# Gated attention with a routed expert layer: one wait on counts dropped for the first batch's scatters, and VectorE's root of the variance moved ahead of the low halves of the expert weights

## The chip, the cores and the metric

The kernel runs on 1 core of one Trainium2 chip. The metric is the time on the device in microseconds (us). The engines are TensorE (PE in the profile; PEld is its weight load), VectorE (DVE), ScalarE (ACT), GpSimd (POOL) and SyncE (SP). Each has its own queue of instructions, and semaphores order the engines among each other. An instruction that finishes can count a semaphore up, and another engine's instruction waits until the count is reached.

## What is computed

Eight batches of 512 tokens with 256 channels. A layer norm gives xn. One branch is an attention over channels, the other a mixture of experts (32 experts, 8 groups of which 3 are kept, 6 experts for each token) with a shared expert:

```python
xn = _layernorm(x, axis=-1)
s = _L0_attn_ref(xn, Wq, Wk, Wv, Wo)         # scores of channels x channels, softmax, times V, times Wo
g = _silu(_L0_ffn_ref(xn, gate, w1, w2, w3, sw1, sw2, sw3))
x = x + s * g
# in _L0_ffn_ref: y = sum over experts of ce * (silu(x @ w1.T) * (x @ w3.T)) @ w2.T, plus the shared expert
```

## The kernel before, in words

The program has two stages. In the **first stage** it goes batch by batch (b = 0 to 7). For each batch it does the norm, the attention, the shared expert, the choice of the six experts of each token and the slot of each copy of a token in a table in DRAM (`slots_d`). GpSimd then copies the tokens to their slots: 24 scatters for a batch (4 tiles of tokens times 6 ranks), 192 in all, each an indirect DMA of 128 rows. In the **second stage** the experts run over pairs of slot tiles, the results go back to `slots_d`, and gathers bring them together again.

The order on each engine in the first stage is written out by hand. What matters here, with the names of the semaphores:

- **TensorE, batch(b)**: shared_up(0); product `s_a_ps`; shared_up(1) (`s_ab_ps`); turn(b+1) (`s_xt_ps`, line 685); product `s_s_ps` (scores); gate(b+1) (`s_lg_ps`, line 698); half 0 of the shared expert's output (`s_y_ps`, line 726); product with Wo (`s_r_ps`, line 710); half 1 (`s_y_ps`, line 726); wait for ScalarE's copy of r; product with V's weights (`s_m_ps`, line 710); gram(b+1) (`s_g_ps`, line 732); count(b+1) (`s_cnt`, lines 704 and 705); wait for ScalarE's copy of m; the attention's output (`s_at_ps`, line 726).
- **ScalarE, batch(b)**, in its later part: split_high(b+1) (line 539; it waits until the scatters of batch b-1 have landed, because they read the buffer that it writes); y half 0 (line 598); copy of r (line 602); y half 1 (line 598) and its DMA; normal(b+2, 0) (line 527; it waits for `s_rstd`, which VectorE counts in moved_mean); copy of m (line 610); normal(b+2, 1); copy of the gram (line 568); copies of the output (line 619); high_weights(b).
- **VectorE, batch(b)**: the two hidden products (line 1044); the maximum of the scores; spread_of(b+2); then route(b+1), split_low(b+1), low_weights(b-1) (line 1050: 12 instructions), spread_root(b+2) (lines 887 to 890), moved_mean (line 898), place(b+1) (lines 947 to 989; it waits for `s_cnt` of b+1 and ends with the slots of b+1, `s_slots`), weigh(b+1).
- **GpSimd** waits for `s_slots` of the batch, for the zeros that SyncE writes into the batch's slots (`s_first_pads`, `s_pads`), and for `s_split` of the tile. Before scatter n of a batch it calls `let_pass(b, n)`, which for some n waits until TensorE has reached a count: n = 2 `s_lg_ps`, 4 `s_y_ps`, 7 `s_r_ps`, 9 `s_y_ps`, 11 `s_m_ps`, 13 `s_cnt`, 15 `s_at_ps`, 17 `s_ab_ps`, 19 `s_a_ps`, 21 `s_xt_ps`. No data of the scatter depends on these waits.

Of the kernel before, what the change touches and what calls it, by code (L numbers as in the profile page):

```python
# [80 lines left out]
def turns(p):  # L81

    return sum(q <= p for q in PE_PAIRS)
# [10 lines left out]
def gated_attention_moe(nc, x, wq, wk_, wvT, wo, gwT, wexp, sw13T, sw2T, out):  # L94
    with ExitStack() as ctx:
# [29 lines left out]
        def chunks(v, c=HC):  # L125
            return v.rearrange("p (c n) -> p c n", c=c)
# [175 lines left out]
        def weights_of(b, low):  # L302
            return w16[:, b * (EB * 2 * WEXP):(b + 1) * (EB * 2 * WEXP)].rearrange(
                "p (e c) -> p e c", e=EB)[:, :, low * WEXP:(low + 1) * WEXP]

        def raw_weights(b):
            return w_all[:, (b + 1) * (EB * WEXP):(b + 2) * (EB * WEXP)].rearrange("p (e c) -> p e c", e=EB)
# [14 lines left out]
        def rank_of(at):  # L322

            return at - at % TOP_K + TOP_K - 1 - at % TOP_K
# [118 lines left out]
        @block.gpsimd  # L443
        def _(pool):
            pool.memset(ident[:], 0.0).then_inc(s_const, 1)
            pool.memset(pad[:], 0.0).then_inc(s_const, 1)
            pool.memset(tri[:], 1.0).then_inc(s_const, 1)
            pool.memset(ones[:], 1.0).then_inc(s_const, 1)
            for r in (restart, restart4, restart8):
                pool.memset(r[:], 1.0).then_inc(s_const, 1)  # L450
            pool.iota(pair_i[:], pattern=[[2 * P, EARLY]], base=3 * P, channel_multiplier=0)
            pool.iota(tile_i[:], pattern=[[P, 3]], base=0, channel_multiplier=3 * P).then_inc(s_const, 1)
            pool.wait_ge(s_const, 8)
            pool.affine_select(out=ident[:], in_=ident[:], compare_op=ALU.not_equal, fill=1.0,
                               base=0, pattern=[[-1, P]], channel_multiplier=1).then_inc(s_const, 1)

            pool.affine_select(out=tri[:], in_=tri[:], compare_op=ALU.is_gt, fill=0.0,
                               base=0, pattern=[[1, P]], channel_multiplier=-1).then_inc(s_const, 1)
            for r, n in ((restart, 1 + E), (restart4, 1 + TB), (restart8, 1 + GROUPS)):
                pool.memset(r[:].rearrange("p (t e) -> p t e", e=n)[:, :, 0:1], 0.0).then_inc(s_const, 1)  # L460


            def let_pass(b, n):

                nxt = b + 1 < B
                due = {4: (s_y_ps, 2 * b + 1), 7: (s_r_ps, b + 1), 9: (s_y_ps, 2 * b + 2),
                       11: (s_m_ps, b + 1), 15: (s_at_ps, 2 * b + 2)}
                if nxt:
                    due.update({2: (s_lg_ps, b + 2), 13: (s_cnt, b + 2), 17: (s_ab_ps, HC * b + HC + 1),
                                19: (s_a_ps, b + 2), 21: (s_xt_ps, 2 * b + 6) if b + 2 < B else (s_a_ps, b + 2)})  # L470
                else:
                    due[2] = (s_s_ps, b + 1)
                if n in due:
                    pool.wait_ge(*due[n])

            for b in range(B):
                pool.wait_ge(s_slots, b + 1)
                if b >= 1:
                    pool.wait_ge(s_pads[b], 16)
                for t in range(TB):  # L480
                    pool.wait_ge(s_split, b * TB + t + 1)
                    if b == 0:
                        pool.wait_ge(s_first_pads[t], 16)
                    for k in range(TOP_K):
                        at = b * BATCH_ROWS + t * TOP_K + k
                        let_pass(b, t * TOP_K + k)
                        pool.indirect_dma_start(slots_d[:, :], bass.IndirectOffsetOnAxis(ap=slot_at[:, at:at + 1], axis=0),  # L487
                                                split[b % XN_RING][:, t, :], None).then_inc(s_disp[b % XN_RING], 16)


            for k in range(XN_RING):
                pool.wait_ge(s_disp[k], 16 * BATCH_ROWS * (B // XN_RING))
            pool.sem_inc(s_scattered, 1)
            stored = 0
            for at in range(GATHERS):
                pages = at + E
                complete = min(-(-pages // 2), PAIRS)
                for pair in range(stored, complete):
                    pool.wait_ge(s_store[pair % DEEP], 16 * (pair // DEEP + 1))
                stored = complete  # L500
                if at >= GATH_RING:
                    pool.wait_ge(s_acc, at - GATH_RING + 1)
                ahead = at // 2 + 18 + SOON
                if at % 2 == 0:
                    pool.wait_ge(s_ehT_ps, min(ahead, PAIRS))
                else:
                    pool.wait_ge(s_eT_ps, turns(min(ahead + SOON + 1, PAIRS - 1)))
                pool.indirect_dma_start(gath[:, at % GATH_RING, :], None, slots_d[:, :],  # L508
                                        bass.IndirectOffsetOnAxis(ap=slot_at[:, rank_of(at):rank_of(at) + 1], axis=0)
                                        ).then_inc(s_gath[at % GATH_RING], 16)  # L510
# [354 lines left out]
        def _(dve):  # L865
# [8 lines left out]
            def spread_of(b):  # L874
                dve.wait_ge(s_x[b], 16)
                for t in range(TB):
                    ins = dve.bn_stats(stats[:, t, :], rows_of(b)[:, t * H:(t + 1) * H])  # L877
                then(ins)
                if b >= 1:
                    dve.wait_ge(s_xn, b * TB)  # L880
                for t in range(TB):
                    ins = dve.bn_aggr(mv[:, t, :], stats[:, t, :])
                ins.then_inc(s_var, 1)
# [13 lines left out]
            def moved_mean():  # L897
                dve.scalar_tensor_tensor(shift[:], mv[:, :, 0], -1.0, rstd[:], ALU.mult, ALU.mult).then_inc(s_rstd, 1)
# [133 lines left out]
            def table_row():  # L1032
                dve.wait_ge(s_table_ps, 1)
                dve.tensor_copy(w_packed.bitcast(I16), ps[0:1, 5, 0:2 * WORDS]).then_inc(s_tables, 1)
# [7 lines left out]
            def hidden(b, m):  # L1042
                dve.wait_ge(s_silu, b * HC + m + 1)
                dve.scalar_tensor_tensor(hT_s[:, m, :], ps[:, 5 + 2 * m, :], 1.0 / (X_UP * W_UP), silu_s[m],
                                         ALU.mult, ALU.mult).then_inc(s_h, 1)

            def low_part(low, raw, high):
                for c in range(WEXP // PART):
                    part_of = slice(c * PART, (c + 1) * PART)
                    ins = dve.scalar_tensor_tensor(low[:, part_of], raw[:, part_of], W_UP, high[:, part_of],  # L1050
                                                   ALU.mult, ALU.subtract)
                ins.then_inc(s_wlo, 1)

            def low_weights(b):
                dve.wait_ge(s_whi, b + 1)
                for e in range(EB):
                    low_part(weights_of(b, 1)[:, e], raw_weights(b)[:, e], weights_of(b, 0)[:, e])
# [6 lines left out]
            def batch(b):  # L1064
                hidden(b, 0)
                hidden(b, 1)
                dve.wait_ge(s_s_ps, b + 1)
                dve.tensor_reduce(mx[:], chunks(ps[:, 0, :]), AX_X, ALU.max).then_inc(s_mx, 1)
                dve.wait_ge(s_mx, b + 1)
                dve.tensor_scalar(nmx[:], mx[:], -SCALE, None, ALU.mult).then_inc(s_nmx, 1)  # L1070
                if b == 0:
                    weigh(0)
                if b + 2 < B:
                    spread_of(b + 2)
                elif b + 2 == B:
                    full_pairs()
                dve.wait_ge(s_ex, b * HC + HC)
                dve.reciprocal(rinv[:], rsum[:]).then_inc(s_ri, 1)
                if b == B - 1:
                    low_weights(b - 1)  # L1080
                    page_table()
                    low_weights_last(0)
                    table_row()
                    low_weights_last(1)
                    return
                route(b + 1)
                split_low(b + 1)
                if b >= 1:
                    low_weights(b - 1)
                if b + 2 < B:  # L1090
                    spread_root(b + 2)
                    moved_mean()
                place(b + 1)
                weigh(b + 1)

# [105 lines left out]
```

## Time and profile before

| what | us |
|---|---|
| median of 3 runs (lowest to highest) | 686.68 (683.47 to 690.63) |
| profiled execution, its own time | 691.99 |
| span of the profiled execution | 690.2 |
| TensorE, VectorE, ScalarE, GpSimd busy | 548.6, 472.2, 359.1, 383.4 |
| TensorE's mean granted clock, as a share | 0.922 |

All times in the rows below are of the profiled execution, counted from the start of its span. What lies around the span is 1.8 us. A row of the timeline gives start, duration, engine, line, operation, what is written and read, how many instructions were merged into the row, and in brackets how long the engine stood idle before it and which work ended that ("issue" when the profile shows nothing that it waited for, "remote" when the release isn't one that the profile can place).

### The profile page before, as it was taken

How to read it: one execution, taken by the hardware profiler on the slowest of the kernel's cores; microseconds unless marked ns; L12 is line 12 of the kernel's file. 1: busy time of each engine (PE TensorE's matmuls, PEld its weight loads, DVE VectorE, ACT ScalarE, POOL GpSimd, SP SyncE). 2: the span in 40 equal slices, each digit the busy share in tenths (PEclk: the TensorE clock that was granted, in tenths of full speed). 3: DMA queues.
4: the chain of work that ended last, by engine and by line, in shares of the span. 5: the costliest groups of instructions: out<-in, count | busy, mean ns of one | idle time of the engine just before them, and what ended most of it. 6: DMA issues, size and time to landing. Idle time of an engine off the chain costs nothing.

```text
span 690.2 us, 14473 instructions
## 1 busy us (share of the span) xinstructions
PE 548.6 (79%) x4095; PEld 446.7 (65%) x4095; DVE 472.2 (68%) x1443; ACT 359.1 (52%) x606; POOL 383.4 (56%) x402
## 2 busy tenths in 40 slices
PE   7789696979697978437999889888888889888830
PEld 6566575756576765326999777777777777677620
DVE  6968687877788877722454567667677667667765
ACT  5546464546464644224655656556556556556421
POOL 1156667676666766753003556556565556565662
PEclk9889798998898999868999999999999999999975
DMA  9999996858393532754888888888888988888764
GB/s 320 416 354 347 366 334 227 285 214 298 130 334 113 207 117 91 230 150 122 201 217 262 290 280 283 280 280 285 290 272 292 279 279 267 290 276 286 226 198 141
DMA packets 111288, 174.80 MB, mean 253 GB/s; under 512 B 25072, under 2 KB 68848, under 8 KB 110320
## 3 DMA queue, kind: packets, MB, share of 16 engines
q1 hardware_dynamic: 87280, 108.29, 47.4%
q0 software_dynamic: 18432, 50.36, 23.2%
q10 hardware_dynamic: 5504, 15.24, 6.4%
q8 instruction: 40, 0.66, 0.4%
q14 instruction: 32, 0.26, 0.1%
HBM read 78.41 MB, written 92.27 MB: 247 GB/s over the span
## 4 chain that ended last, share of the span: by engine, by line
PE 53%; DVE 21%; issue 15%; another core or an unknown queue 6%; ACT 4%; DMA 1%; DVEq 0%; SPq 0%; ACTq 0%
PE ps L835 17%; PE ps L857 8%; PE ps L726 7%; PE ps L710 6%; PE ps L818 6%; PE ps L718 4%; DVE sw L1133 3%; PE ps L845 3%; PE ps L732 2%; DVE w_all L1050 2%; DVE work L1152 2%; DVE work L1159 1%; DVE stats L877 1%; DVE early L1141 1%
## 5 line engine op out<-in xcount | busy, mean ns | idle before, releaser
L508 POOL DMA_INDIRECT early<-slots_d,slot_at x192 | 186.6, 972 | 178.0 <-DMA slots_d<-early 56.6
L487 POOL DMA_INDIRECT slots_d<-early,slot_at x96 | 96.9, 1009 | 75.0 <-issue 25.7
L487 POOL DMA_INDIRECT slots_d<-work,slot_at x96 | 97.7, 1018 | 45.1 <-issue 26.5
L835 PE MATMUL ps<-w_all,xnT 128*128 x798 | 102.9, 275 | 15.9 <-issue 13.6
L835 PEld LDWEIGHTS ps<-w_all,xnT 128*128 128x128 f16 x798 | 71.4, 98 | 36.3 <-issue 24.6
L647 ACT ACTIVATE xnT<-ps 128x1024 f16<-128x1024 f16 x67 | 68.8, 1029 | 46.6 <-PE ps L818 28.0
L668 ACT ACTIVATE early<-ps 128x512 f32<-128x512 f32 x112 | 67.3, 602 | 46.6 <-remote 30.8
L818 PE MATMUL ps<-ident,work 128*128 128x128 f16 x796 | 66.7, 222 | 24.9 <-issue 24.8
L1159 DVE CAST work<-ps 128x256 f16<-128x256 f32 x75 | 31.6, 422 | 75.0 <-remote 45.0
L1133 DVE SCALAR_TENSOR_TENSOR sw<-early,wk,sw 128x256 f32<-128x256 f32 x160 | 77.7, 486 | 3.5
L818 PEld LDWEIGHTS ps<-ident,work 128*128 128x128 f16 x796 | 54.6, 99 | 28.8 <-issue 26.4
L653 ACT ACTIVATE work<-ps 128x256 f32<-128x256 f32 x112 | 43.9, 393 | 55.6 <-remote 37.9
L857 PE MATMUL ps<-w_all,work 128*128 x447 | 62.6, 277 | 0.9 <-issue 0.9
L1152 DVE SCALAR_TENSOR_TENSOR work<-ps,work 128x256 f32<-128x256 f32 x112 | 46.5, 416 | 20.4 <-ACT work L653 19.0
L710 PE MATMUL ps<-early,work 128*128 128x256 f32 x128 | 39.4, 462 | 25.8 <-ACT work L533 18.9
L835 PE MATMUL ps<-w_all,sw 128*128 x396 | 50.6, 274 | 8.3 <-issue 8.0
L710 PEld LDWEIGHTS ps<-early,work 128*128 128x128 f32 x128 | 28.6, 231 | 34.7 <-ACT work L533 21.0
L726 PE MATMUL ps<-work,early 128*128 128x256 f32 x128 | 34.7, 432 | 17.7 <-issue 13.8
L857 PEld LDWEIGHTS ps<-w_all,work 128*128 128x128 f16 x447 | 43.9, 99 | 6.3 <-issue 1.5
L835 PEld LDWEIGHTS ps<-w_all,sw 128*128 128x128 f16 x396 | 35.4, 98 | 18.6 <-issue 12.7
L647 ACT ACTIVATE sw<-ps 128x1024 f16<-128x1024 f16 x33 | 34.0, 1032 | 20.9 <-remote 15.4
L718 PE MATMUL ps<-xnT,sw 128*128 128x512 f16 x192 | 44.0, 379 | 0.0
(164 smaller groups left out, 989.4 us busy)
## 6 DMA issues: line engine op xcount, KB each, us to landing
slots_d<-early SPq DMA_DIRECT2D x112, 256.0 KB
work<-slots_d SPq DMA_DIRECT2D x100, 256.0 KB
slots_d<-pad SPq DMA_DIRECT2D x7, 3072.0 KB
w_all<-in_wexp ACTq DMA_DIRECT2D x7, 1536.0 KB
slots_d<-work SPq DMA_DIRECT2D x1, 5120.0 KB, 19.2
s_all<-in_x SPq DMA_DIRECT2D x8, 512.0 KB, 6.3
ysh_d<-work ACTq DMA_DIRECT2D x8, 512.0 KB
early<-ysh_d SPq DMA_DIRECT2D x32, 128.0 KB
```

The lines of the kernel that those rows point to most:

```text
L487: pool.indirect_dma_start(slots_d[:, :], bass.IndirectOffsetOnAxis(ap=slot_at[:, at:at + 1], axis=0), split[b % XN_RING][:, t, :], None).t ...
L508: pool.indirect_dma_start(gath[:, at % GATH_RING, :], None, slots_d[:, :], bass.IndirectOffsetOnAxis(ap=slot_at[:, rank_of(at):rank_of(at) ...
L647: act.activation(x_halves[n % 3], turned_pair(p), ACT.Copy).then_inc(s_eT, 1)
L668: act.activation(y_e[:, p % DEEP, :], ps[:, 2 + p % 2, :], ACT.Copy, scale=1.0 / W_UP).then_inc(s_ey, 1)
L710: mm = pe.matmul(ps[:, bank, m * H:(m + 1) * H], lhs[:, k, m * P:(m + 1) * P], rhs[:, k, :], start=(k == 0), stop=(k == HC - 1))
L718: mm = pe.matmul(ps[:, 4 + 2 * m + w, :], sw13[:, w_low, w, k, m * P:(m + 1) * P], xnT16[:, x_low, k, :], start=(n == 0 and k == 0), stop= ...
L726: mm = pe.matmul(ps[:, bank + n, t * H:(t + 1) * H], lhs[:, k, at:at + P], rhs[:, k, :], start=(k == 0), stop=(k == HC - 1))
L818: mm = pe.transpose(turned_pair(p)[:, at:at + P], slot16[:, at_slot(p) + h, low, c * P:(c + 1) * P], ident16[:])
L835: mm = pe.matmul(ps[:, 5 + p % 2, h * 2 * I:(h + 1) * 2 * I], turned_x(p)[:, x_low * HC + k, h * P:(h + 1) * P], w16[:, bass.ds(at + (w_lo ...
L857: mm = pe.matmul(ps[:, 2 + p % 2, h * H:(h + 1) * H], hT_e[p % 3][:, h_low, h, :], w16[:, bass.ds(at + (w_low * WEXP + HC * 2 * I), H)], s ...
L1133: dve.scalar_tensor_tensor(acc[:, k, :], gath[:, at % GATH_RING, :], wk[:, rank_of(at):rank_of(at) + 1], ysh_l[k] if at % TOP_K == 0 else ...
L1152: dve.scalar_tensor_tensor(h_e[p % 2], up(p)[:, :, 1, :], 1.0 / (X_UP * W_UP), silu_e[p % 2], ALU.mult, ALU.mult).then_inc(s_eh, 1)
```

## The change

`low_weights(b - 1)` on VectorE moves behind `spread_root(b + 2)` and `moved_mean()`. And GpSimd's `let_pass` does nothing in batch 0: its ten waits on counts of TensorE are left out there; in batches 1 to 7 they stay.

```diff
@@ -470,7 +470,7 @@
                 else:
                     due[2] = (s_s_ps, b + 1)
-                if n in due:
+                if b >= 1 and n in due:
                     pool.wait_ge(*due[n])
@@ -1085,11 +1085,11 @@
                 route(b + 1)
                 split_low(b + 1)
-                if b >= 1:
-                    low_weights(b - 1)
                 if b + 2 < B:
                     spread_root(b + 2)
                     moved_mean()
+                if b >= 1:
+                    low_weights(b - 1)
                 place(b + 1)
                 weigh(b + 1)
```

## Rows read from the trace of the kernel before

**Rows 1.** The page: DMA share in 40 slices; the chain that ended last, by engine.
```profile
DMA  9999996858393532754888888888888988888764
...
PE 53%; DVE 21%; issue 15%; another core or an unknown queue 6%; ACT 4%; DMA 1%; DVEq 0%; SPq 0%; ACTq 0%
```

**Rows 2.** Timeline of GpSimd over batch 0's scatters and the first of batch 1.
```profile
28.69 1.42 POOL L487 DMA_INDIRECT slots_d<-early,slot_at  x1 [25.64 <-DVE slot_at L989]
...
35.22 0.96 POOL L487 DMA_INDIRECT slots_d<-early,slot_at  x1 [0.31 <-issue]
...
44.23 1.00 POOL L487 DMA_INDIRECT slots_d<-early,slot_at  x1 [3.42 <-PE ps L710]
...
68.52 0.96 POOL L487 DMA_INDIRECT slots_d<-work,slot_at  x1 [0.30 <-issue]
```

**Rows 3.** Timeline of batch 0's end: TensorE, then ScalarE, then VectorE.
```profile
40.46 3.49 PE L710 MATMUL ps<-early,work 128*128 128x256 f32 x8 [3.42 <-ACT work L533]
...
45.51 1.89 PE L710 MATMUL ps<-work,early 128*128 128x256 f32 x8
...
50.80 3.67 PE L726 MATMUL ps<-work,early 128*128 128x256 f32 x16
...
43.98 0.60 ACT L602 ACTIVATE work<-ps 128x512 f32<-128x512 f32 x1 [2.15 <-PE ps L710]
...
58.80 0.18 DVE L989 TENSOR_TENSOR slot_at<-in_order,in_page 128x24 int32<-128x24 int32 x1
```

**Rows 4.** Timeline of batch 1: TensorE, then ScalarE, then GpSimd.
```profile
71.49 1.99 PE L710 MATMUL ps<-early,work 128*128 128x256 f32 x8 [1.19 <-issue]
73.32 1.89 PE L726 MATMUL ps<-early,work 128*128 128x256 f32 x8
79.56 3.78 PE L710 MATMUL ps<-work,early 128*128 128x256 f32 x8 [4.36 <-issue]
...
64.44 1.08 ACT L544 ACTIVATE early<-ps 128x512 f32<-128x512 f32 x2 [2.23 <-remote]
...
78.91 0.60 ACT L602 ACTIVATE work<-ps 128x512 f32<-128x512 f32 x1 [3.87 <-remote]
...
79.16 1.73 POOL L487 DMA_INDIRECT slots_d<-work,slot_at  x1 [1.96 <-remote]
```

**Rows 5.** Timeline of batch 7: TensorE, then ScalarE, then GpSimd.
```profile
281.07 1.89 PE L726 MATMUL ps<-early,work 128*128 128x256 f32 x8
282.79 1.89 PE L710 MATMUL ps<-work,early 128*128 128x256 f32 x8
298.48 5.90 PE L726 MATMUL ps<-work,early 128*128 128x256 f32 x16 [13.80 <-issue]
...
281.27 0.60 ACT L602 ACTIVATE work<-ps 128x512 f32<-128x512 f32 x1 [1.60 <-PE ps L710]
292.00 0.60 ACT L598 ACTIVATE work<-ps 128x512 f32<-128x512 f32 x1 [10.13 <-remote]
...
297.83 0.60 ACT L610 ACTIVATE work<-ps 128x512 f32<-128x512 f32 x1 [3.22 <-remote]
...
272.08 0.96 POOL L487 DMA_INDIRECT slots_d<-early,slot_at  x1 [1.84 <-remote]
...
298.07 0.95 POOL L487 DMA_INDIRECT slots_d<-work,slot_at  x1 [3.38 <-remote]
```

**Rows 6.** Timeline of batch 4 around VectorE's root: VectorE, ScalarE, TensorE.
```profile
187.55 4.11 DVE L1050 SCALAR_TENSOR_TENSOR w_all<-w_all 128x256 f16<-128x256 f32 x12
...
192.56 1.09 ACT L527 ACTIVATE early<-s_all,shift,rstd 128x256 f32<-128x256 f32 x2 [3.29 <-DVE shift L898]
...
194.19 3.72 PE L726 MATMUL ps<-work,early 128*128 128x256 f32 x16 [0.26 <-ACT work L610]
```

**Rows 7.** Timeline of ScalarE in batch 3.
```profile
154.74 1.09 ACT L527 ACTIVATE early<-s_all,shift,rstd 128x256 f32<-128x256 f32 x2 [5.02 <-DVE shift L898]
156.19 0.60 ACT L610 ACTIVATE work<-ps 128x512 f32<-128x512 f32 x1 [0.36 <-remote]
```

## The prediction, made before the change was built or run

> **What bounds the kernel now.** I read the chain that ended last first: TensorE has 53% of it, VectorE 21%, and 15% is "issue", in which an engine stood still and the profile names no reason [rows 1]. The change touches the first stage alone, which ends near 312 us, when TensorE starts on the expert rows. So the question is what sets TensorE's pace in that stage. I read it next in the timeline of each engine, batch by batch. TensorE's order closes one batch with: product r, output half 1, ScalarE's copy of r, product m, gram, count, ScalarE's copy of m, attention output. Any delay of a copy there is a delay of everything behind it.
>
> Batch 0 runs cleanly. Product r ends at 43.95 (40.46 + 3.49), ScalarE copies it at 43.98, and GpSimd's next scatter, which had waited 3.42 us for that same count, goes at 44.23 [rows 2, 3]. Batch 1 doesn't. Product r ends at 73.48 and half 1 at 75.21, yet ScalarE's copy of r starts at 78.91, released by something the profile calls remote, and TensorE stands idle 4.36 us [rows 4]. GpSimd ended the scatter before at 77.20 (79.16 - 1.96), stopped for the same count, and got it at 79.16. So TensorE's count reached the others 5.4 us late, and 1.7 us after GpSimd stopped issuing. Batch 7 shows it larger: half 1 ends at 282.96 by its row and ScalarE sees it at 292.00, 9.0 us late, with GpSimd still issuing; product m ends at 284.68 and is seen at 297.83, 3.1 us after GpSimd stopped at 294.69 (298.07 - 3.38). TensorE lost 13.80 us [rows 5]. The timeline has this in all seven batches from 1 to 7, with 1.6 to 3.1 us from GpSimd's stop to the count. What goes with it is how many scatters GpSimd has issued without a pause: counts mostly arrive at once behind up to six of them (batch 7's r even behind eight: copied at 281.27, with a run that began at 272.08), and every TensorE count completed behind nine or more came late. I read the rows thus: **a long unbroken run of scatters holds back TensorE's counts, and a pause lets them pass.** The rows show the coincidence, not the cause.
>
> Here the Trainium skill speaks against this reading. SBUF — State Buffer, section "Who interferes with whom", says that a DMA never contends with a compute engine and that PE and ACT never wait on anyone; by that rule the runs of scatters cost TensorE nothing, and leaving the waits out in batch 0 is free. The trace doesn't settle it, since Perfetto Trace Analysis, section "Summary: the profiler window per engine type", says that TensorE's end is an estimate and the semaphore's propagation isn't shown. I keep the rule as the rival "no hold" below, whose time comes from rows.
>
> **The change, part by part.** *The root on VectorE.* The 12 instructions of line 1050 take 4.11 us together [rows 6]; behind the change the root and the shift, five small instructions, come 4.1 us earlier and low_weights some 1 us later (five starts 0.2 us apart). Only counts move; no work is added. place waits for TensorE's count behind both in all batches, so it isn't later, and high_weights of the batch needs the low halves only 6 us afterwards. What gains is ScalarE's normal(b+2, 0), which stands ahead of the copy of m. It waited for the shift in five batches, up to 5.02 us [rows 7]. But the copy of m then waits for product m as well. In batch 3 the copy still waited 0.36 us for TensorE's count, so an earlier shift gives nothing [rows 7]; batches 1 and 2 are the same. In batch 4 it is VectorE that comes last, and TensorE lost 0.26 us [rows 6]; in batch 5 TensorE didn't wait. Sum: 0.3 us. The bounds are 0 below (nothing gets slower) and, if the held counts were not held, some 4.1 us for batch 3, which is what the shift moves. I take 0.3, since the rows of batches 1 to 3 say that the count came last.
>
> *The scatters of batch 0.* Ten waits leave GpSimd's queue; what was queued behind them are the scatters. They start at 28.69 in either kernel, one each 1.27 us (0.96 and 0.31 between, [rows 2]). 24 of them end at 28.69 + 24 x 1.27 = 59.2 us; now the last ends just ahead of batch 1's first, at 68.52 [rows 2]. Batch 1 can't start before its slots, ready at 58.98 [rows 3], so GpSimd comes level with the others instead of 9.5 us behind. That lag is paid back in two ways.
>
> The gain comes in batch 1. Level with TensorE, GpSimd stops at n = 2, 4, 7, 9 for counts that aren't there yet, and the runs stay under four scatters. Then product m starts behind half 1 at 75.2 and not at 79.56: 4.4 us. ScalarE's copies of the turned rows waited 2.23 us for a late count [rows 4]; the table load and the scores behind them give back 1.5 of it, by my estimate (the scores' own count was ready 0.6 us before). The first part helps here: with product m done that early, the copy of m would wait for a shift that comes behind the 4.11 us of low halves in the old order. By batch 2 GpSimd is back at a lag of 7 us, since scatter 21 of batch 1 waits for a turn that is in TensorE's batch 2; I count 1 us there and nothing from batch 3 on, where all waits are as they were. Gain: 4.4 + 1.5 + 1.0 = 6.9, with the first part 7.2 us. Bounds: 4.4 (batch 1's product m alone) and 9.5 (the whole lag).
>
> The price comes in batch 0. Product r completes at 43.95 behind 12 unbroken scatters, in a run of 24. The nearest rows are batch 7's, with the longest run (18): the first count 9.0 us late with GpSimd issuing, the next held until it stops [rows 5]. On batch 0: r is seen at 53.0, copied at 53.6, product m ends at 53.6 + 1.9 = 55.5 and is seen only 2 us after the stop, at 61.2; the copy ends at 61.8, and the attention output starts there and not at 50.80: **11.0 us later**. All behind it moves along, the slots of batch 1 included. Low bound 0 (no hold) or 2.3 us (each count 3 us late). High bound: r itself held until 61.2, then copy 0.6 and 5.3 us from product m to the output (50.80 - 45.51, [rows 3]): 67.1, so 16.3 us.
>
> DMA is the other resource. It is nine tenths busy in the first six slices, that is up to 103 us [rows 1]. By 60 us five scatters more are queued than before, 128 KB each; what is queued with them (zeros of batch 1, rows of batch 3, weights) is needed 10 us or more after it lands now. I count nothing, and nothing at the end of the stage either: the last scatters are tied to counts of batches 6 and 7.
>
> **Sum.** 11.0 - 7.2 = +3.8 us against the profiled execution, 691.99 + 3.8 = 695.8. That execution lies 5.3 us above the median of the runs, whose own spread is 7 us; against the median, **690.5 us**.
>
> **Rivals.** *(A) Held to the end:* the count of r gets out only when GpSimd stops, as in batch 1, where r's count had to wait for the pause. +16.3 - 7.2 = +9.1: 695.8 us. It decides this way if nothing gets through between 44 and 59 us. For it: in five of seven batches the second late count came only behind the stop. Against it: the 9.0 us of batch 7. *(B) No hold:* the lateness has another cause (the DMA load, say), and batch 0 costs nothing. -7.2: 679.5 us. For it: no row shows a held count in batch 0, and the skill's rule above. Against it: each release follows the stop. *(C) Small holds:* 2.3 us or so in batch 0, -4.9: 681.8 us. *(D) The change does nothing:* the hold costs what the lag cost, or batch 1 falls behind again at once for the zeros or the slots: 686.7 us.
>
> **How the numbers follow.** The forecast has 0.36, (A) 0.26, (B) 0.17, (C) 0.11, (D) 0.10. The range goes from (B) to just above (A), 679.5 to 697, since the bounds of both terms lie within; the forecast's own is 688 to 693.5. One per cent is 6.9 us, and that is about what a measurement of this kernel tells from no change. Faster by over 1% (below 679.8) has half of (B) and a little from a larger gain: 0.12. Slower by over 1% (above 693.6) has most of (A) and an edge of the forecast: 0.28. Within 1%: 0.60.
>
> **What the new profile would show.** GpSimd's 24 first scatters unbroken from 28.7 to 59 us and then idle until the slots of batch 1. ScalarE's copy of r of batch 0 (line 602) late against the end of product r, near 53 (forecast), 61 (A), or 44 us (B); the copy of m (line 610) near 61 us. In batch 1 the copy of r within 0.1 us of product r's end and no idle time of TensorE ahead of product m. Line 887 ahead of line 1050 in batches 1 to 5, and ScalarE's waits for the shift gone. Wrong would be: TensorE's counts prompt in batch 0; batch 1's counts as late as before; or another end of batch 7, which I hold to be unchanged.

## The result, and the profile after

The changed kernel takes **698.43 us** (median of 4 runs, 695.48 to 700.38), the kernel before, run beside it, 688.65 us (4 runs, 683.47 to 692.09). The ratio is **1.0144**, with a 95% interval of 1.0096 to 1.0192: slower by 9.8 us. The profiled execution took 695.48 us with a span of 693.7 us. It is the quickest of the four, and that of before, 691.99 us, lies at the upper end of its own runs, so the two traces are only 3.5 us apart; what follows compares places in them, not their ends. The ratios below leave out the executions that took over 1.5% longer than the fastest of their kernel (920.21 us with own pauses, 793.21 us without any waits, one of 694.86 us of before).

The chain that ended last, by engine, has more of what the profile can't name than in [rows 1]:

```profile
PE 57%; DVE 17%; issue 11%; another core or an unknown queue 9%; ACT 4%; DMA 1%; DVEq 0%; ACTq 0%; SPq 0%
```

Timeline of batch 0's end after the change: TensorE, ScalarE, VectorE, then GpSimd (start, duration, then in brackets the idle time ahead and what ended it).

```profile
46.59 1.89 PE L710 MATMUL ps<-work,early 128*128 128x256 f32 x8
...
63.48 6.74 PE L726 MATMUL ps<-work,early 128*128 128x256 f32 x16 [11.43 <-ACT work L610]
...
51.83 0.22 PE L705 MATMUL ps<-sel,tri 128*128 128x128 bf16 x1
...
44.26 0.60 ACT L602 ACTIVATE work<-ps 128x512 f32<-128x512 f32 x1 [2.44 <-issue]
49.51 0.60 ACT L598 ACTIVATE work<-ps 128x512 f32<-128x512 f32 x1 [4.65 <-remote]
...
62.83 0.60 ACT L610 ACTIVATE work<-ps 128x512 f32<-128x512 f32 x1 [11.09 <-remote]
...
63.06 0.39 DVE L949 COPY counts<-ps 128x128 f32<-128x128 f32 x1 [15.07 <-remote]
...
58.59 0.96 POOL L487 DMA_INDIRECT slots_d<-early,slot_at  x1 [0.30 <-issue]
71.07 1.03 POOL L487 DMA_INDIRECT slots_d<-work,slot_at  x1 [11.52 <-DVE slot_at L989]
```

Product m of batch 0 ends at 48.48 (46.59 + 1.89). ScalarE, which waits for that count alone, starts the copy at 62.83, 14.35 us late and 3.3 us after GpSimd ended its 24th scatter (58.59 + 0.96 = 59.55). VectorE sees the count of line 705, whose matmul ended at 52.05, at 63.06: the two come out together, 11.0 and 14.35 us late. TensorE stands idle 11.43 us, and the attention output starts at 63.48 and not at 50.80 [rows 3], **12.7 us later**. Then comes something the prediction has no term for. The same 16 matmuls take 6.74 us and not 3.67. These are the granted clock and the rest of the columns in windows of the changed kernel (stretch, its length, busy time of each engine, PEclk, DMA share, GB/s):

```profile
48.00:52.00 4.00, 4.00 (x21) 3.32 (x19) 0.00 (x0) 1.70 (x3) 3.04 (x4) 1.00 1.07 393
...
63.00:70.00 7.00, 6.52 (x16) 5.18 (x17) 6.47 (x25) 2.49 (x5) 0.00 (x0) 0.53 1.06 356
```

TensorE had the full clock before the idle time and 0.53 of it, that is nearly all at the lower level (1.2 GHz), in the 7 us behind. So batch 0 ends at 70.22 and not at 54.47: 15.7 us later.

Batch 1 gives a part back. Timeline of the changed kernel, TensorE and ScalarE:

```profile
88.44 2.71 PE L726 MATMUL ps<-early,work 128*128 128x256 f32 x8
90.99 1.89 PE L710 MATMUL ps<-work,early 128*128 128x256 f32 x8
...
96.28 3.67 PE L726 MATMUL ps<-work,early 128*128 128x256 f32 x16
...
88.69 0.60 ACT L602 ACTIVATE work<-ps 128x512 f32<-128x512 f32 x1 [1.56 <-issue]
```

Product r's count is read at 88.69, prompt, and product m follows half 1 at once; [rows 4] has 4.36 us of idle time there. The output of batch 1 started at 87.37 before the change and starts at 96.28: +8.9, so 6.8 of the 15.7 us are back. No steady gain comes after that: the outputs of batches 2 to 6 are 9.3 (131.41), 8.7, 5.1, 9.5 and 10.7 us (270.14) later than before, since each batch's holds differ between the two traces. In this trace batch 7's hold is small (1.44 us of idle time where [rows 5] has 13.80), its output starts only 1.1 us later, and stage 2 starts at 318.11 against 312.21:

```profile
299.55 3.72 PE L726 MATMUL ps<-work,early 128*128 128x256 f32 x16 [1.44 <-issue]
...
318.11 1.87 PE L818 MATMUL ps<-ident,work 128*128 128x128 f16 x16 [14.73 <-issue]
```

The root's order is as the diff says (VectorE in batch 3; [rows 7] has ScalarE waiting for that shift):

```profile
160.41 0.16 DVE L898 SCALAR_TENSOR_TENSOR shift<-mv,rstd 128x4 f32<-128x4 f32 x1
160.49 4.16 DVE L1050 SCALAR_TENSOR_TENSOR w_all<-w_all 128x256 f16<-128x256 f32 x12
```

### The profile page after: what moved, and what is told of

It is laid out like the page before. It is cut to its first block, busy times and chain, and to the rows that moved or that the text cites. A ratio compares the mean times of both kernels' runs of the same rounds, so it can differ in the third digit from the quotient of the medians.

```text
span 693.7 us, 14473 instructions
## 1 busy us (share of the span) xinstructions
PE 547.8 (79%) x4095; PEld 449.2 (65%) x4095; DVE 472.3 (68%) x1443; ACT 359.5 (52%) x606; POOL 381.6 (55%) x402
## 3 DMA queue, kind: packets, MB, share of 16 engines
q0 software_dynamic: 18432, 50.36, 23.4%
## 4 chain that ended last, share of the span: by engine, by line
PE 57%; DVE 17%; issue 11%; another core or an unknown queue 9%; ACT 4%; DMA 1%; DVEq 0%; ACTq 0%; SPq 0%
PE ps L835 21%; PE ps L857 10%; PE ps L818 7%; PE ps L710 5%; PE ps L726 4%; PE ps L845 3%; PE ps L718 3%; DVE w_all L1050 2%; PE ps L732 2%; DVE stats L877 1%; DVE sw L1133 1%; DMA s_all<-in_x 1%; DVE gains L1023 1%; DVE mx L1068 1%
## 5 line engine op out<-in xcount | busy, mean ns | idle before, releaser
L835 PE MATMUL ps<-w_all,xnT 128*128 x798 | 102.1, 274 | 15.0 <-issue 13.2
L710 PE MATMUL ps<-early,work 128*128 128x256 f32 x128 | 42.8, 494 | 29.2 <-ACT work L533 24.2
L710 PEld LDWEIGHTS ps<-early,work 128*128 128x128 f32 x128 | 30.8, 248 | 38.8 <-ACT work L533 26.9
```

Source lines behind the costliest of these rows:

```text
L710: mm = pe.matmul(ps[:, bank, m * H:(m + 1) * H], lhs[:, k, m * P:(m + 1) * P], rhs[:, k, :], start=(k == 0), stop=(k == HC - 1))
L835: mm = pe.matmul(ps[:, 5 + p % 2, h * 2 * I:(h + 1) * 2 * I], turned_x(p)[:, x_low * HC + k, h * P:(h + 1) * P], w16[:, bass.ds(at + (w_lo ...
```

## The experiments

**Two conditions.** The 16 runs below were made in five groups, each on one chip with the kernel before timed beside it. Before took 695.3, 688.7, 590.2, 589.9 and 690.1 us in them. The difference of 100 us isn't the kernel's: the first, third and fourth group ran on the same chip. I call the groups of 690 us "with the hold" and those of 590 us "without" it: in the latter no engine's wait in any kernel's first stage is put down to "remote", and a copy of ScalarE that stood waiting for TensorE starts within 0.05 us of the product's end by its row. One trace was kept of each kernel in each group, so what differs between two traces can belong to the execution as well as to the kernel. Theory: a long unbroken run of GpSimd's scatters holds TensorE's counts until GpSimd pauses, and that is the change's whole loss. Rivals: the bytes of the scatters do it; only a wait for TensorE can end it; the loss comes from elsewhere.

### First group (with the hold): which part, and what ends a hold

Root alone: the diff's second half. Scatters alone: its first half. Two waits and own pauses: the change, with

```diff
+                if (b >= 1 or n in (7, 11)) and n in due:      # two waits
                     pool.wait_ge(*due[n])
...
+                if b == 0 and n in (8, 16):                    # own pauses
+                    pool.wait_ge(s_disp[0], 16 * n)
```

The second makes GpSimd wait for its own scatters' landing and for nothing of TensorE.

> VectorE's root moved ahead of the low halves, and nothing else. Theory 'hold' (an unbroken run of scatters on GpSimd holds back TensorE's counts until GpSimd pauses): the root is no part of the loss; 0 to 1 us faster than the kernel before, and the copy of m of batch 0 near 48 us as before. Rival 'root' (the new order on VectorE costs the time): slower by about the 9.8 us of the whole change.

> The first batch's scatters without waits, VectorE in the old order. Theory 'hold': slower than before by 9.8 us and some 1 to 2 us more, since in batch 1 the copy of m then waits for the shift; the copy of m of batch 0 near 62.8 us, 3 us behind GpSimd's stop. Rival 'root': the time of the kernel before.

> The whole change, but batch 0 keeps two of its ten waits, on the counts of product r (n = 7) and product m (n = 11). Theory 'hold': GpSimd pauses near 38 to 44 us, the count of m then completes behind three scatters and is prompt, so the 11 us idle time of TensorE ahead of batch 0's output is gone; but 17 scatters follow without a pause, and the turn's counts of batch 1 (57 to 62 us) are held to about 68 us: 0 to 4 us slower than before. Rival 'load' (the earlier scatters load the DMA engines, and what TensorE waits for is late for that): most of the 9.8 us stays, since the scatters are only 5 us later than in the changed kernel.

> The whole change, but in batch 0 GpSimd waits twice, at n = 8 and n = 16, until all its own scatters so far have landed: pauses that have nothing to do with TensorE. Theory 'hold': runs of eight with a pause of some 6 us between let every count of batch 0 pass; the copy of m of batch 0 starts within 3 us of 48 us, TensorE's 11 us of idle time is gone, and the time is within 3 us of the kernel before. Rival 'the wait itself' (only a wait on that count gets it delivered in time): the copy of m stays near 60 us and the time near the changed kernel's.

*Root alone* measured 1.0000 (0.9978 to 1.0022): nothing. *Scatters alone* measured 1.0140 (1.0111 to 1.0169), as much as the whole change and not the 1 to 2 us more that were expected, with half 1 and m held as there:

```profile
50.28 0.60 ACT L598 ACTIVATE work<-ps 128x512 f32<-128x512 f32 x1 [5.61 <-remote]
...
62.97 0.60 ACT L610 ACTIVATE work<-ps 128x512 f32<-128x512 f32 x1 [10.47 <-remote]
```

So the ten waits of batch 0 (one line of the code, hence the title's "one wait") are the whole loss, and rivals that need the root's move fall.

*Two waits* measured 1.0087 (1.0055 to 1.0118), 6.0 us and not 0 to 4. That much of the loss stays is what the rival "load" said; but the copies of r and m are prompt, which it didn't allow. But the second wait finds its count already there, so from the first one on GpSimd runs into batch 1 without a pause, and the next counts are held instead (ScalarE, then GpSimd):

```profile
49.16 0.57 ACT L610 ACTIVATE work<-ps 128x512 f32<-128x512 f32 x1
...
60.87 0.60 ACT L619 ACTIVATE s_all<-ps 128x512 f32<-128x512 f32 x1 [8.06 <-remote]
...
44.46 1.03 POOL L487 DMA_INDIRECT slots_d<-early,slot_at  x1 [6.59 <-PE ps L710]
...
68.03 0.96 POOL L487 DMA_INDIRECT slots_d<-work,slot_at  x1 [0.30 <-issue]
```

Between 44.46 and 68.99 it issued 19 scatters; ScalarE stood idle 8.06 us for the count of the output's first half and 10.01 us for that of the second, which it read at 71.48, 15.7 us after the output's matmuls ended. Protecting two counts moved the hold to the next.

*Own pauses* measured 1.0070 (1.0047 to 1.0092), 4.9 us where at most 3 were expected. Timeline of its GpSimd and ScalarE (here m's copy has line 612, half 1's line 600, split_high line 541):

```profile
45.89 0.96 POOL L489 DMA_INDIRECT slots_d<-early,slot_at  x1 [6.75 <-DMA slots_d<-early,slot_at]
...
63.04 0.96 POOL L489 DMA_INDIRECT slots_d<-early,slot_at  x1 [6.92 <-DMA slots_d<-early,slot_at]
...
83.41 0.97 POOL L489 DMA_INDIRECT slots_d<-work,slot_at  x1 [0.31 <-issue]
...
79.11 1.06 ACT L541 ACTIVATE early<-early 128x1024 f16<-128x1024 f32 x1 [8.59 <-DMA slots_d<-early,slot_at]
...
87.25 0.60 ACT L600 ACTIVATE work<-ps 128x512 f32<-128x512 f32 x1 [5.78 <-remote]
```

In batch 0 the 11 us of idle time are gone (m's copy at 48.4), though GpSimd waits for nothing of TensorE: a pause of its own does it. The price is 13.7 us of stopping, which puts batch 0's last scatters later. ScalarE's split_high in batch 1 waits 8.59 us for them to land, so its copy of r starts at 80.88, 8.3 us after product r ended, and TensorE stands idle 7.23 us ahead of product m: a loss of this run that is no hold. The run of scatters from 63.04 to 84.38 holds half 1 of batch 1 besides, until 87.25, 2.9 us after that run ends.

### Second group (with the hold): bytes, and how far it goes

Thin rows: the change, with batch 0's scatters writing 64 bytes a row into a table of their own; it leaves out batch 0's rows for the experts. No waits: `let_pass` waits nowhere. Earlier waits: the root's move and batch 0's waits, with batches 1 to 6 waiting two scatters earlier. Cores of the edits:

```diff
+                        wide = 16 if b == 0 else H                                   # thin rows
...
-                if n in due:                                                         # no waits
-                    pool.wait_ge(*due[n])
...
+                    due = {0: (s_lg_ps, b + 2), 2: (s_y_ps, 2 * b + 1), 5: (s_r_ps, b + 1), 7: (s_y_ps, 2 * b + 2),
+                           9: (s_m_ps, b + 1), 11: (s_cnt, b + 2), ...
```

> The whole change, but batch 0's 24 scatters write 64 bytes of each row (into a table of their own) and not 1 KB: the same instructions, indices and number of descriptors, a sixteenth of the bytes. It leaves out batch 0's rows for the experts. Theory 'hold' (issuing on GpSimd is what holds the counts back): the copy of m of batch 0 still stands 8 us or more behind its place in the kernel before, near 60 us, and the time is within 4 us of the changed kernel's. Rival 'load' (the bytes of the early scatters load the DMA engines): the copy of m near 48 us and the time within 3 us of the kernel before.

> The whole change, and let_pass waits for nothing in any batch: GpSimd stops only for a batch's slots. Theory 'hold': each batch from 1 on then has a run of 24 as batch 0 has in the changed kernel; GpSimd is level at each batch's start, the copy of m is held until about 3 us behind its stop, and each batch costs some 8 to 12 us more: 40 to 80 us slower than before. Rival 'only the first batch' (something of the first 60 us, its zeros and loads, makes the loss): within 5 us of the changed kernel.

> The root moved, batch 0 with all its waits, and in batches 1 to 6 each wait two scatters earlier, with one more on the scores' count: GpSimd has fewer scatters behind it when the count of r comes. Theory 'hold': the run ahead of r falls from 8 to 6 or less, and its lateness of 5 us in batches 1 and 2 goes: 5 to 20 us faster than before. Rival 'scatters late': ScalarE's split_high waits for scatters that now land later and gives it back: same or slower.

*Thin rows* measured 1.0104 (1.0060 to 1.0149). With a sixteenth of the bytes the hold is what it was, so the bytes of these scatters are not its cause; their instructions and, within 2%, the packets of the program's software DMA queue (18048 and 18432) stay as they were, so these two aren't told apart:

```profile
49.00 0.60 ACT L600 ACTIVATE work<-ps 128x512 f32<-128x512 f32 x1 [3.99 <-remote]
...
63.03 0.60 ACT L612 ACTIVATE work<-ps 128x512 f32<-128x512 f32 x1 [11.80 <-remote]
```

*No waits* measured **1.1482** (1.1436 to 1.1527), some 100 us and not 40 to 80. In every batch one count or more is held for some 10 to 20 us; in batches 1 to 6 it is the count of r, and not of m as expected. The end of batch 2, TensorE, ScalarE and GpSimd (lines two lower than in the change):

```profile
135.09 3.78 PE L708 MATMUL ps<-early,work 128*128 128x256 f32 x8 [4.98 <-issue]
...
156.22 3.78 PE L708 MATMUL ps<-work,early 128*128 128x256 f32 x8 [14.36 <-ACT work L600]
...
155.56 0.60 ACT L600 ACTIVATE work<-ps 128x512 f32<-128x512 f32 x1 [13.36 <-remote]
...
151.26 1.03 POOL L485 DMA_INDIRECT slots_d<-early,slot_at  x1 [0.30 <-issue]
```

Product r ends at 138.87 and is read at 155.56, 16.7 us late and 3.3 us after GpSimd's last scatter (152.29). From this trace, of the execution of 793.21 us, I take the places alone.

A load on the DMA engines, the rival "load" of the expectations, isn't what goes with a hold. In this kernel r of batch 5 is held for 18.7 us while the DMA share is 0.28 (286 to 306 us). In the change without the hold (fourth group) the share is 1.04 between 30 and 60 us, as in the change with it, and every count is prompt.

*Earlier waits* measured 1.0023 (0.9997 to 1.0049), no change where 5 to 20 us of gain were expected. ScalarE's copy of r comes 2 to 5 us earlier in six of the seven batches behind the first (276.93 in batch 7 against 281.27, [rows 5]), but the count of r is still 4.4 us late in batch 2, and batch 7's m waits for the end of GpSimd's run all the same, at 296.55 against 297.83, now behind 20 scatters and 16.2 us late:

```profile
276.93 0.60 ACT L607 ACTIVATE work<-ps 128x512 f32<-128x512 f32 x1 [1.60 <-PE ps L715]
...
296.55 0.60 ACT L615 ACTIVATE work<-ps 128x512 f32<-128x512 f32 x1 [11.80 <-remote]
```

The rival had the time right, but its reason hardly shows: split_high waited 2.4 us for landed scatters in the whole stage, against 2.1 us before.

### Third group: the condition had changed

Last batches: the earlier waits, with two more at the end of batch 6 and four in batch 7. Short spacers: the change, with one tiny fill on GpSimd and a wait for its own count before every third scatter of batch 0. Long spacers: 30 such fills before the ninth and seventeenth.

```diff
+            def space(times):
+                for _ in range(times):
+                    spaced["n"] += 1
+                    pool.memset(tile_i[:], 0).then_inc(s_ln, 1)
+                    pool.wait_ge(s_ln, spaced["n"])
```

> As the kernel with earlier waits (batch 0 with all its waits, root moved, batches 1 to 6 two scatters earlier), and besides in batches 6 and 7: scatters 22 and 23 of batch 6 wait for the counts of batch 7's output half 0 and of its r, and batch 7's scatters wait at n = 0 for half 1, n = 1 for m, n = 4 for the attention output, n = 5 for the turned page table. Theory 'hold': in batch 7 GpSimd's run is 18 long when m is counted, and that costs 10 to 14 us; with a stop ahead of it the copy of m of batch 7 comes near 281 us and not 297 us, and the whole is 5 to 12 us faster than before. Rival 'late scatters': the last scatters end some 5 us later, TensorE's second stage starts beside them with its counts held, and the gain is given back: within 3 us of before.

> The whole change, and in batch 0 a tiny fill on GpSimd's own cores ahead of every third scatter (eight in all, 0.1 to 0.2 us each): the run of scatters is broken by another instruction, but hardly in time. Reading 'time without issuing' (a stop of 2 us or more is what lets the counts pass): nothing changes, the copy of m near 62 us. Reading 'any other instruction': the counts of batch 0 pass and the copy of m is near 48 us, the time that of the kernel before or better.

> The whole change, and in batch 0 GpSimd does small fills in a chain ahead of scatters 8 and 16, some 3 us or more each time: it issues no scatter in that time but waits for no other engine and for no transfer. Theory 'hold, until issuing stops': the counts pass in those gaps, r and half 1 are prompt or come out in the first gap, m within 3 us of its end or in the second gap; the copy of m between 48 and 54 us and the loss at most half of the 9.8 us. Rival 'a wait is needed': copy of m near 62 us and the full loss.

They measured 1.0029 (1.0017 to 1.0042), 0.9934 (0.9912 to 0.9957) and 1.0054 (1.0036 to 1.0071). None of these tests what it was made for: before took 590.2 us, and no kernel of the group had a held count to protect. Last batches and long spacers then show only the cost of stopping GpSimd; short spacers, whose last scatter of batch 0 starts at 59.70 us, a microsecond after the change's (58.59), show about the change without a hold, 3.8 us **faster** than before.

### Fourth group: the change itself without the hold

The change as it is, short spacers, no waits and root alone again.

> The change as it is. Theory (the hold of TensorE's counts by GpSimd's long run is the whole loss): where the kernel before takes about 690 us, batch 0's attention output starts at 63 to 64 us after 11 us of idle and the time is 1.010 to 1.019 of before; where the kernel before takes about 590 us (no count held), the counts m and half 1 are read within 0.5 us of their matmuls, the output starts by 53, batch 1 earlier than before, and the time is 0.990 to 0.996 of before. Rival (the change costs something else, such as the order of batch 0's scatters against batch 1's or VectorE's new order): at or above 1.000 in both conditions.

> The change with a fill of about 0.12 us on GpSimd before every third scatter of batch 0. With the hold absent both theories say the same as for the change alone, within 0.2%. With the hold present: if any instruction of GpSimd that waits for its own count lets the held counts pass, m is read before 50 us and the time is 0.990 to 1.002 of before; if only a stop of some microseconds does, m is read at 62 to 63 as in the change and the time is 1.010 to 1.019.

> No scatter of any batch waits for a count of TensorE. Theory: with the hold present 1.14 to 1.15 of before, as measured; with it absent there is nothing for the waits to protect, and the time is 0.98 to 1.01 of before, no count read more than 0.5 us late. Rival (the waits also keep GpSimd's transfers out of others' way): slower by more than 2% in both conditions.

> The root's move alone. Both theories: within 0.3% of before with the hold present, as measured; with it absent the same, so that any gain of the change there belongs to batch 0's scatters. Rival (the root's move carries the gain where no count is held): 0.990 to 0.996 there.

Before took 589.88 us (20 runs). *The change* measured **0.9942** (0.9923 to 0.9960), short spacers 0.9941 (0.9921 to 0.9962), *no waits* **0.9858** (0.9833 to 0.9882), root alone 1.0019 (1.0004 to 1.0033). The kernel that loses 14.8% with the hold gains 1.4% without it. The change in this condition, TensorE and ScalarE of batch 0:

```profile
45.33 1.89 PE L710 MATMUL ps<-work,early 128*128 128x256 f32 x8
...
50.62 3.67 PE L726 MATMUL ps<-work,early 128*128 128x256 f32 x16
...
47.66 0.57 ACT L610 ACTIVATE work<-ps 128x512 f32<-128x512 f32 x1
...
268.49 1.86 PE L818 MATMUL ps<-ident,work 128*128 128x128 f16 x16 [9.61 <-issue]
```

m is read at 47.66, 0.4 us after its product ended (ScalarE was busy until then) and behind some 15 unbroken scatters, and the output runs at the full clock. Stage 2 starts at 268.49, in root alone at 271.82: so stage 1 has 3.3 of the 3.7 us between the two spans. Where it comes from is suggested by the chains that ended last, here of root alone:

```profile
PE 50%; POOL 18%; DVE 17%; issue 9%; DMA 3%; ACT 1%; DVEq 0%; POOLq 0%; ACTq 0%
```

and here of the change:

```profile
PE 57%; DVE 23%; POOL 8%; issue 7%; ACT 2%; DMA 2%; POOLq 0%; DVEq 0%; ACTq 0%
```

Without the hold GpSimd's scatters are in the chain, and batch 1's start earlier (60.2 against 66.6 us); that this shortens the chain is my reading, no run isolates it. "Another core or an unknown queue", 6% in [rows 1], 9% after the change and 19% in no waits with the hold, is absent here.

### Fifth group (with the hold): the spacers where they matter

> The change with a fill of about 0.12 us before every third scatter of batch 0. If the kernel before takes about 690 us here: m read before 50 us and 0.990 to 1.002 of before, if any short wait of GpSimd lets counts pass; m read at 62 to 63 us and 1.010 to 1.019, if only a stop of microseconds does. If the kernel before takes about 590 us: 0.992 to 0.996, as twice before, and the question stays open.

> The change with two rests of some 4 us (30 fills in a chain) before the ninth and the seventeenth scatter of batch 0. If the kernel before takes about 690 us here: m read before 51 us by both theories, and 1.000 to 1.008 of before, since batch 0's scatters end 9 us later and run into batch 1's. If it takes about 590 us: 1.004 to 1.007, as measured.

Before took 690.12 us (19 runs). *Short spacers* measured 1.0080 (1.0048 to 1.0112). Neither expectation held: m (line 620 here) is read at 58.69, 10.2 us late, with GpSimd still issuing.

```profile
58.69 0.60 ACT L620 ACTIVATE work<-ps 128x512 f32<-128x512 f32 x1 [9.09 <-remote]
...
59.34 5.45 PE L736 MATMUL ps<-work,early 128*128 128x256 f32 x16 [7.26 <-issue]
...
59.20 0.97 POOL L497 DMA_INDIRECT slots_d<-early,slot_at  x1 [0.28 <-POOL tile_i L481]
```

So fills of 0.1 us don't clear a hold, and the hold of m didn't last until the stop. The counts behind it did: those of gram and of line 705 are read at 63.06 and 63.11, 2.9 us after GpSimd's run ended at 60.17. *Long spacers* measured **1.0010** (0.9972 to 1.0049), within the expected 1.000 to 1.008:

```profile
39.24 4.69 POOL L481 MEMSET tile_i<- 128x3 int32 x30
...
44.02 0.60 ACT L612 ACTIVATE work<-ps 128x512 f32<-128x512 f32 x1 [2.14 <-PE ps L720]
...
47.88 0.58 ACT L620 ACTIVATE work<-ps 128x512 f32<-128x512 f32 x1
...
50.84 3.67 PE L736 MATMUL ps<-work,early 128*128 128x256 f32 x16
```

Two rests of some 5 us that have nothing to do with TensorE restore m's promptness, the clock and the time of before. Of what the waits do in batch 0, a rest does the same.

## Why the prediction was wrong

The forecast was 690.5 us with a range to 697.0, and "within 1%" had 0.60; measured were 698.43 us and +1.4%, which had 0.28. The mechanism, a hold until after GpSimd's stop, was the right one in this condition, and the place too, but for the way of r and half 1 to it (below). **The step that failed is the price of batch 0: sized at +11.0 us, it measured 15.7 us (12.7 us of lateness of the output and 3.1 us of its lower clock)**, and the sum came out at +3.8 where +9.8 (6.6 to 13.2 by the interval) was measured.

- *Release after the stop.* I took 2 us; it was 3.3 us, and GpSimd stopped at 59.55 rather than 59.2. Together 1.6 us more: the output started 12.7 us late. The rows of before had 1.6 to 3.1 us, with 3.1 behind the longest run [rows 5], and I took the middle for a still longer one.
- *The clock.* The term was missing. Behind 11.43 us of idle time the output took 6.74 us instead of 3.67: 3.1 us. [Rows 5] showed this at 13.80 us of idle time, where the same 16 matmuls took 5.90 us, and I read only the bracket of that row.
- *The way to it* was told wrong, with no effect on the sum. r wasn't held behind 12 unbroken scatters (read at 44.26; forecast 53.0), so "every count completed behind nine or more came late" isn't a rule. Half 1 was held to 49.51, and m, complete at 48.48 and not at 55.5, waited for the stop anyhow; that the error cost nothing is luck. Rival (A) gave nearly the measured sum (+9.1) by a mechanism that didn't occur.
- *The gain of batch 1* was forecast at 5.9 us and measured 6.8. Batch 2's 1.0 us did not come (+8.9 became +9.3). GpSimd didn't stop at n = 4 there as told: its runs in batch 1 were of 5, 6 and 8 scatters after the first two, and not under four.
- *The root:* 0.3 us forecast; root alone measured 1.0000 and 1.0019. That it helps batch 1 fits the scatters alone, where the copy of m of batch 1 starts at 95.4 us against 93.3, though the output starts no later there (96.00 against 96.28); in the time of the kernel it can't be told apart.
- *Batch 7* was held to be unchanged. Its hold differs from trace to trace, and whether that is the kernel or the execution isn't shown: ScalarE's first copy of its output starts at 301.58 in the changed kernel's trace, at 313.1 in that of the scatters alone and at 302.3 before.

Put right, the sum is 11.0 + 1.6 + 3.1 - 6.8 = +8.9 us, inside the interval. Its terms are read from the two traces, so it says where the loss lies and is no test of the mechanism; that is the experiments' part. **Rival (B), no hold,** is what the third and fourth group show: the change gains 0.58% there (3.4 us; I had 7.2). The prediction had the two as rivals about one chip, and both exist, the first wherever before takes 690 us. The rule of the Trainium skill (SBUF — State Buffer, section "Who interferes with whom") that PE and ACT never wait on anyone stands among rules on the ports of SBUF and says nothing of counts. Read as widely as the prediction read it, it fits the traces of the 590 us groups; where before takes 690 us the trace disagrees with that reading, with 11.09 us of ScalarE and 11.43 us of TensorE spent on a count that was long complete by the row of its product.

**What stays open:** what the hold is, whether GpSimd's issuing itself or the packets of its scatters make it, and why a chip has it in one group and not in another; whether anything else was at work on the chip is not on record. Also why short spacers released m 4 us earlier than the plain change, and why r gets through behind 12 scatters in batch 0 where that of batch 1 before the change came 5.4 us late behind seven.

## What to carry to other kernels

A wait that no data needs can be what paces a queue: before taking it out, compare, at the far end of the queue's other long unbroken stretches, when a product ends and when its reader starts. Price an idle gap of TensorE with the matmuls behind it at their lower clock, not by its length alone. And time such a change in more than one session: here its sign is 1.4% one way and 0.6% the other, and no version that was run beats the kernel before in both.

## What was not expected of the hardware

- Two conditions of the same kernel on the same chip, 695 and 590 us. Root alone was run and traced in both: of the difference some 41 us lie in stage 1 (it ends at 312.54 or 271.82 us) and some 64 in stage 2 (381 or 317 us). There, too, counts seem to be late. Costliest groups of ScalarE on the page of the changed kernel (busy, mean ns of one, idle time before and its main releaser), with the hold:

```profile
L647 ACT ACTIVATE xnT<-ps 128x1024 f16<-128x1024 f16 x67 | 69.0, 1032 | 51.3 <-remote 28.6
...
L653 ACT ACTIVATE work<-ps 128x256 f32<-128x256 f32 x112 | 44.1, 394 | 50.8 <-remote 34.6
```

and without it:

```profile
L647 ACT ACTIVATE xnT<-ps 128x1024 f16<-128x1024 f16 x67 | 68.2, 1019 | 11.3 <-PE ps L818 11.3
...
L653 ACT ACTIVATE work<-ps 128x256 f32<-128x256 f32 x112 | 43.1, 384 | 33.8 <-PE ps L835 33.6
```

GpSimd's scatters are over by then; its gathers run there. Whether these hold counts as the scatters do wasn't tried.
- With the hold: it doesn't depend on the bytes (64 B rows held m until 63.03), it held a count of r for 16.7 us in the kernel without waits, it can end for several counts together (after the change ScalarE sees m at 62.83 and VectorE the count at 63.06), and rests of 5 us on GpSimd prevent it.
